# A message-passing kernel: last products and sums in two halves, fourteen groups of three, tile 1 centred ahead of the weights

## What is computed

```python
h = jnp.maximum(_layernorm(x, axis=-1), 0.0)
x_i = h[src]; x_j = h[dst]
m_ij = jax.nn.relu(jnp.concatenate([x_i, x_j], axis=1) @ W.T + b)
out = x + jax.ops.segment_sum(m_ij, src, num_segments=50000)
```

## Time and profile before

| what | value |
|---|---|
| median of 3 runs | 733.67 us (732.49 to 734.08) |
| profiled execution, its own time | 734.02 us |
| its span, first to last instruction | 732.0 us |
| mean granted clock of TensorE | 0.994 |
| busy: PE, DVE, ACT, POOL | 707.6, 628.2, 342.4, 375.0 us |

### The profile page before, as it was taken

The page is one execution under the profiler, slowest core; times in us unless marked ns, Lnnn a source line. Parts: engine busy times, 40 slices in busy tenths (PEclk is TensorE's granted clock), DMA queues, the critical chain, the costliest instruction groups (busy, mean ns, idle before and its releaser), DMA issues.

```text
span 732.0 us, 12594 instructions
## 1 busy us (share of the span) xinstructions
PE 707.6 (97%) x3466; PEld 586.6 (80%) x3466; DVE 628.2 (86%) x1868; ACT 342.4 (47%) x646; POOL 375.0 (51%) x306
## 2 busy tenths in 40 slices
PE   3999999999999999999999999999999999999995
PEld 2778888888888888888888888888888888888874
DVE  5879999889989989988988998988888888888973
ACT  4444553544445455354445535445444445454441
...
GB/s 259 383 391 358 391 372 339 374 357 353 391 339 380 343 370 371 341 386 347 349 192 141 140 144 150 152 133 162 137 143 146 137 138 147 159 154 160 86 86 73
DMA packets 36042, 182.46 MB, mean 249 GB/s; under 512 B 7019, under 2 KB 7343, under 8 KB 33049
## 3 DMA queue, kind: packets, MB, share of 16 engines
...
## 4 chain that ended last, share of the span: by engine, by line
PE 94%; DMA 2%; DVE 2%; issue 1%; another core or an unknown queue 0%; POOL 0%; ACT 0%; SPq 0%; DVEq 0%; POOLq 0%
PE z_ps L635 24%; PE z_ps L644 24%; PE z_ps L641 24%; PE ht_ps L618 11%; PE agg_ps L650 5%; PE agg_ps L651 5%; DMA ring<-w_chunks 1%; DMA xg<-x,node_i 1%; DVE ht_lo L313 1%; DVE m_lo L385 0%; DMA node_i<-node_cols 0%; POOL out L236 0%; DVE zb L334 0%; POOL xg L213 0%
## 5 line engine op out<-in xcount | busy, mean ns | idle before, releaser
L213 POOL DMA_INDIRECT xg<-x,node_i x196 | 211.3, 1078 | 245.8 <-PE ht_ps L618 201.2
L635 PE MATMUL z_ps<-w_hi,ht_hi 128*128 128x512 f32 x784 | 315.9, 403 | 1.7 <-DVE zb L323 1.5
L644 PE MATMUL z_ps<-w_hi,ht_lo 128*128 128x512 f32 x784 | 308.9, 394 | 0.0
L641 PE MATMUL z_ps<-w_lo,ht_hi 128*128 128x512 f32 x784 | 307.1, 392 | 0.0
L498 ACT CAST ht_hi<-ht_ps 128x512 fp32r<-128x512 f32 x194 | 104.7, 590 | 299.3 <-PE ht_ps L618 290.9
L236 POOL DMA_INDIRECT out<-ring,add_i x98 | 158.1, 1613 | 104.6 <-DMA out<-ring,add_i 53.3
L644 PEld LDWEIGHTS z_ps<-w_hi,ht_lo 128*128 128x128 f32 x784 | 147.8, 189 | 32.8 <-DVE ht_lo L451 0.2
L635 PEld LDWEIGHTS z_ps<-w_hi,ht_hi 128*128 128x128 f32 x784 | 148.1, 189 | 31.7 <-issue 2.8
L641 PEld LDWEIGHTS z_ps<-w_lo,ht_hi 128*128 128x128 f32 x784 | 148.1, 189 | 30.0
L313 DVE TENSOR_TENSOR ht_lo<-ht_ps,ht_hi 128x512 fp32r<-128x512 f32 x194 | 124.6, 684 | 8.1 <-ACT ht_hi L498 5.6
L505 ACT ACTIVATE xg<-xg,neg_mean 128x512 f32<-128x512 f32 x194 | 129.2, 720 | 2.0 <-DVE neg_mean L287 2.0
...
## 6 DMA issues: line engine op xcount, KB each, us to landing
out<-x SPq DMA_DIRECT2D x125, 800.0 KB
...
out<-ring,add_i POOLq DMA_INDIRECT x98
row_lanes<-src_rows ACTq DMA_DIRECT2D x49, 4.0 KB
...
```

Of the source, the lines that this page charges most:

```text
L213: nc.gpsimd.indirect_dma_start(out=xg[:, b, s, :], out_offset=None, in_=x, in_offset=bass.IndirectOffsetOnAxis(ap=node_i[:, column:column ...
L635: nc.tensor.matmul(z_ps[s][:, :], hi, w_hi[:, c, :], start=(k == 0), stop=False)
L641: nc.tensor.matmul(z_ps[s][:, :], hi, w_lo[:, c, :], start=False, stop=False)
L644: last = nc.tensor.matmul(z_ps[s][:, :], lo, w_hi[:, c, :], start=False, stop=(k == KD - 1))
```

## The change

- **Start.** VectorE takes the statistics of tile 1 after its first w_lo, ahead of tile 0's low part. ScalarE makes tile 1's deviations and centres it ahead of the high parts of weights 4 to 7. Steps 0 and 1 of both engines are written out in another order. `W_POOL` goes from 5 to 6: VectorE makes six low parts of the weights, POOL two. SyncE waits for the first gather only before the third weight load. The half sums of tile 1 go to the two banks of `agg_ps`, so its products don't wait for zb of tile 0.
- **Groups.** `TRIPLES` goes from 12 to 14, FIRST3 from 60 to 54. Eight steps leave the loops of TensorE and VectorE.
- **End.** The products of tile 97's second side, the last sums and what follows run in two halves of 256 columns, in banks of their own; ScalarE copies the first half to the ring, VectorE the second, and POOL waits for both.

```diff
--- before.py
+++ after.py
@@ -26,18 +26,19 @@
     KD = D // P
     K = SIDES * KD
     EPS = 1e-5
-    TRIPLES = 12
+    TRIPLES = 14
     FIRST3 = TILES - 2 - 3 * TRIPLES
     GROUPS = ([(f, 2) for f in range(0, FIRST3, 2)] + [(f, 3) for f in range(FIRST3, TILES - 2, 3)]
               + [(TILES - 2, 2)])
     W_LOADS = 4
-    W_POOL = 5
+    W_POOL = 6
     XS = 8
     RAMP = 4
     RING = 52
     FIRST_ADD = 56
     ROWS = 4
     LANES = 32
+    HALVES = (slice(0, OUT // 2), slice(OUT // 2, OUT))
     COPY_RUNS = 16
     COPY_ROWS = COPY_RUNS * 25
     COPIES = N // COPY_ROWS
@@ -103,6 +104,8 @@
         ht_ps = [[ps(f"ht_ps{b}{s}", [P, KD * P]) for s in range(SIDES)] for b in range(2)]
         z_ps = [ps(f"z_ps{s}", [P, OUT]) for s in range(SIDES)]
         agg_ps = [ps(f"agg_ps{b}", [P, OUT]) for b in range(2)]
+        last_z = [z_ps[1][:, HALVES[0]], ht_ps[0][0][:, HALVES[0]]]
+        last_agg = [agg_ps[0][:, HALVES[0]], ht_ps[0][1][:, HALVES[0]]]
 
         nodes_loaded = sem("nodes_loaded")
         w_loaded = [sem(f"w_loaded{n}") for n in range(W_LOADS)]
@@ -154,6 +162,10 @@
             pos = (t - FIRST3) % 3
             return pos, t - pos, 3
 
+        def half_sum(t, s):
+
+            return agg_ps[s] if isinstance(t, int) and t == 1 else z_ps[s]
+
         def sums_before(t, b):
 
             pos, first, size = place(t, b)
@@ -171,8 +183,7 @@
             for n in range(W_LOADS):
                 if n == 2:
 
-                    for side in range(SIDES):
-                        sp.wait_ge(first_arrived[side], 16)
+                    sp.wait_ge(first_arrived[0], 16)
                 ks = slice(n * K // W_LOADS, (n + 1) * K // W_LOADS)
                 sp.dma_start(ring[:, ks, :], w_of[:, ks, :]).then_inc(w_loaded[n], 16)
             sp.dma_start(bias_bc[:, :], bias.to_broadcast([P, OUT])).then_inc(bias_loaded, 16)
@@ -230,7 +241,7 @@
                     if group == len(GROUPS) - 1:
                         pool.wait_ge(add_ready, t + 1)
                     if t == TILES - 1:
-                        pool.wait_ge(last_filled, 1)
+                        pool.wait_ge(last_filled, 2)
                     else:
                         pool.wait_ge(ring_filled, t + 1)
                     nc.gpsimd.indirect_dma_start(
@@ -320,7 +331,7 @@
                 if not (isinstance(t, int) and t == 0):
                     dve.wait_ge(mlo_ready, t)
                 dve.wait_ge(half_done, t + 1)
-                nc.vector.scalar_tensor_tensor(out=zb[:, :], in0=z_ps[0][:, :], scalar=rstd[:, q, b, 0:1],
+                nc.vector.scalar_tensor_tensor(out=zb[:, :], in0=half_sum(t, 0)[:, :], scalar=rstd[:, q, b, 0:1],
                                                in1=bias_bc[:, :], op0=ALU.mult, op1=ALU.add).then_inc(half_scaled, 1)
 
             def second_half(t, m):
@@ -331,7 +342,7 @@
                 if not isinstance(t, int):
 
                     dve.wait_ge(stats_done, SIDES * (t + 4))
-                nc.vector.scalar_tensor_tensor(out=zb[:, :], in0=z_ps[1][:, :], scalar=rstd[:, q, b, 1:2],
+                nc.vector.scalar_tensor_tensor(out=zb[:, :], in0=half_sum(t, 1)[:, :], scalar=rstd[:, q, b, 1:2],
                                                in1=zb[:, :], op0=ALU.mult, op1=ALU.add).then_inc(biased, 1)
 
             def same_source(t, m):
@@ -453,28 +464,52 @@
 
             first_moments(0, first_mean)
             first_moments(1, mean_ready)
-            w_low_parts(0, 2)
+            w_low_parts(0, 1)
+            statistics(1, 1)
             first_low_part(0)
-            w_low_parts(2, 3)
+            aggregate(1, 1)
+            w_low_parts(1, KD)
             first_low_part(1)
-            w_low_parts(3, KD)
-            statistics(1, 1)
-            aggregate(1, 1)
             w_low_parts(KD, W_POOL)
+            statistics(2, 2)
+            low_parts(1, 1)
             scales(1, 0)
+            aggregate(2, 0)
             dve.wait_ge(bias_loaded, 16)
+            first_half(0, 0)
+            second_half(0, 0)
+            statistics(3, 3)
+            aggregate(3, 1)
+            low_parts(2, 0)
+            message_low(0, 0)
+            first_half(1, 1)
             dve.wait_ge(consts, 4)
             dve.wait_ge(src_cast, 8)
-            for s in range(0, 3):
-                step(s, s)
+            same_source(0, 0)
+            lanes(0, 0)
+            scales(3, 1)
+            step(2, 2)
             rounds = (FIRST3 - 2) // XS
             with dve.Fori(3, 3 + XS * (rounds - 1) + 1, XS) as s:
                 for d in range(XS):
                     step(s + d, (3 + d) % XS)
-            for s in range(3 + XS * rounds, TILES + 1):
+            for s in range(3 + XS * rounds, TILES):
                 step(s, s % XS)
-            dve.wait_ge(agg_done, TILES)
-            nc.vector.tensor_copy(ring[:, (TILES - 1) % RING, :], agg_ps[0][:, :]).then_inc(last_filled, 1)
+            m, pos = (TILES - 1) % XS, place(TILES - 1, 1)[0]
+            same_source(TILES - 1, m)
+            lanes(TILES - 1, 1)
+            dve.wait_ge(half_scaled, TILES)
+            for h, cols in enumerate(HALVES):
+                dve.wait_ge(last_product, h + 1)
+                nc.vector.scalar_tensor_tensor(out=zb[:, cols], in0=last_z[h], scalar=rstd[:, m // 2 % 2, 1, 1:2],
+                                               in1=zb[:, cols], op0=ALU.mult, op1=ALU.add).then_inc(last_biased, 1)
+                dve.wait_ge(last_high, h + 1)
+                nc.vector.scalar_tensor_tensor(out=m_lo[:, pos, cols], in0=zb[:, cols], scalar=0.0,
+                                               in1=m_hi[:, pos, cols].bitcast(F32), op0=ALU.max, op1=ALU.subtract
+                                               ).then_inc(last_low, 1)
+            dve.wait_ge(last_sum, 2)
+            nc.vector.tensor_copy(ring[:, (TILES - 1) % RING, HALVES[1]], last_agg[1]
+                                  ).then_inc(last_filled, 1)
 
         @block.scalar
         def _(act):
@@ -583,11 +618,16 @@
             first_centre(1, mean_ready)
             first_high_part(0)
             first_high_part(1)
-            w_high_parts(KD, K)
             deviations(1)
             centre(1, 1)
-            for s in range(0, 3):
-                step(s, s)
+            w_high_parts(KD, K)
+            high_parts(1, 1)
+            centre(2, 2)
+            message_high(0, 0)
+            high_parts(2, 0)
+            deviations(3)
+            centre(3, 3)
+            step(2, 2)
             with act.Fori(3, RING - XS, XS) as s:
                 for d in range(XS):
                     step(s + d, (3 + d) % XS)
@@ -603,7 +643,12 @@
                 step(s, s % XS, again=True)
             act.wait_ge(scattered, 16 * (TILES - RING))
             store_sum(TILES - 2, 1, True)
-            step(TILES, TILES % XS, again=True)
+            act.wait_ge(agg_done, sums_before(TILES - 1, 1))
+            for h, cols in enumerate(HALVES):
+                act.wait_ge(last_biased, h + 1)
+                nc.scalar.activation(m_hi[:, place(TILES - 1, 1)[0], cols], zb[:, cols], ACT.Relu).then_inc(last_high, 1)
+            act.wait_ge(last_sum, 1)
+            nc.scalar.copy(ring[:, (TILES - 1) % RING, HALVES[0]], last_agg[0]).then_inc(last_filled, 1)
 
         @block.tensor
         def _(pe):
@@ -622,8 +667,8 @@
             def products(t, b, sides=(0, 1)):
 
                 for s in sides:
-                    if not (isinstance(t, int) and t == 0):
-                        pe.wait_ge(half_scaled if s == 0 else biased, t)
+                    if not (isinstance(t, int) and t < 2):
+                        pe.wait_ge(half_scaled if s == 0 else biased, 1 if isinstance(t, int) and t == 2 else t)
                     early = isinstance(t, int) and t == 0
                     pe.wait_ge(hi_ready if early else lo_ready, SIDES * t + s + 1)
                     for k in range(KD):
@@ -632,16 +677,16 @@
                         lo = ht_lo[:, b, s, k * P:(k + 1) * P]
                         if early:
                             pe.wait_ge(w_hi_ready, c + 1)
-                        nc.tensor.matmul(z_ps[s][:, :], hi, w_hi[:, c, :], start=(k == 0), stop=False)
+                        nc.tensor.matmul(half_sum(t, s)[:, :], hi, w_hi[:, c, :], start=(k == 0), stop=False)
                         if early:
 ...
@@ -657,6 +702,8 @@
                 pe.wait_ge(same_ready, t + 2)
                 if not isinstance(t, int) or t >= 2:
                     pe.wait_ge(ring_filled, t)
+                else:
+                    pe.wait_ge(biased, 2)
                 pe.wait_ge(mlo_ready, t + 2)
                 sum_of(0, ((0, 0), (1, 1)))
                 sum_of(1, ((2, 1),))
@@ -680,17 +727,33 @@
                 pe.wait_ge(ring_filled, t)
                 pe.wait_ge(mlo_ready, t + 1)
                 sum_of(1, ((2, 1),))
-                nc.tensor.matmul(agg_ps[0][:, :], same[:, 1, :], m_hi[:, 1, :], start=True, stop=False)
```

(31 more changed lines are left out.)

11 lines of the change are left out of this document (8 added, 3 removed).

## The result

The changed kernel takes 736.48 us (median of 22 runs, 732.25 to 746.23); the kernel before, on the same chip, 733.76 (22 runs). The ratio is 1.0034 with an interval of 1.0019 to 1.0050: slower by a third of a per cent, outside the forecast range of 729.3 to 733.9. The profiled execution took 736.59 us, with a span of 734.9.

A forecast was written before the change was run, and what follows sets the result against it. TensorE's own instruction stream was taken to bound the middle, VectorE's queue the start, the compute chain the end. Start -2.5, triples +1.37 and halves -0.87 gave -2.0 us: 731.7 us against a median of 733.67, range 729.3 to 733.9.

The forecast's parts named there:

- The start: First 43 us: reordered statistics, centring and loads bring tile 3's products earlier; -2.5 us, bounds -0.5 and -3.7.
- SyncE's line: Start: weight loads about 0.7 us sooner compete with tile 1's and 2's gathers; no gain, possibly a few tenths lost.
- the bound taken for VectorE: Start: tile 2's gather, landing at about 20.1 us, limits VectorE; zb of tile 2 at 37.3 us without a stall.
- The stall: VectorE's uncaused 2.92 us wait before the first loop: taken as 2.0 us, the mean of two cases.
- TensorE's clock: Start: TensorE staying at 1.2 GHz until 23 us costs 0.7 us, of which half is charged.
- The triples: Middle: fourteen groups of three instead of twelve add six sum matmuls on TensorE, uncovered; +1.37 us.
- The add chain's part: POOL's adds: fewer pairs and more triples let add 96 start at 720.8 us and add 97 at 722.6.
- The halves: End: last products in 256-column halves, 0.122 us each, shorten the chain behind from 3.94 to 2.75 us; -0.87 us net.
- rival by which weight loads set the pace: End: each 256-column matmul takes 0.188 us instead of 0.122, making the end +0.9 us; chance 0.08.
- The floor: End: the chain of adds stops any gain beyond 4.4 us, so 729.3 us is the lowest time.
- the slower rival: End: weight loads pace the halves, +2.3 us with the triples, slower if the start gives under 0.8; chance 0.08.
- The start gives little: Rival, start: early statistics delay needed low parts, tile 2 lands later or the stall stays; net 0 to -0.8; chance 0.28.

The follow-up runs named there:

- a1: The change with SyncE waiting again for both first gathers before the third weight load; 733.68 us, ratio 1.0001 to the kernel before.
- c1: A repetition of a1, the same kernel, in another series; 731.85 us, ratio 0.9978 to the kernel before.
- d1: The change itself, run again unaltered in a later series; 741.01 us, ratio 1.0008 to the kernel before.
- a2: The kernel before with only SyncE's wait relaxed to the first gather, as in the change; 733.17 us, ratio 1.0002 to the kernel before.
- b2: As b1, but with the change's SyncE wait for the first gather alone; 731.74 us, ratio 0.9975 to the kernel before.
- d2: The change with tile 1's statistics and aggregation put behind tile 0's low parts on VectorE; 737.51 us, ratio 0.9975 to the kernel before.
- d3: The change with weights 4 to 7 put back ahead of tile 1's centring on ScalarE; 738.27 us, ratio 0.9972 to the kernel before.
- c3: The change with SyncE waiting for tile 0's and tile 1's gathers before the third weight load; 733.77 us, ratio 0.9989 to the kernel before.
- a5: The change with twelve groups of three instead of fourteen; 735.58 us, ratio 1.0027 to the kernel before.
- b1: The change with the whole start of the kernel before, keeping fourteen groups of three and the halves at the end; 731.04 us, ratio 0.9978 to the kernel before.
- d4: The kernel before, unaltered, run once more for another profile; one execution, 739.08 us.
- e1: The kernel before with fourteen groups of three and nothing else; 733.26 us, ratio 0.9986 to the kernel before.
- c2: A repetition of b1, the same kernel, in another series; 731.49 us, ratio 0.9956 to the kernel before.
- e2: A third run of the kernel of b1 and c2, beside e1; 734.40 us, ratio 0.9992 to the kernel before.
- a3: The kernel before with only the last products, sums and copies in two halves, twelve groups of three kept; 733.90 us, ratio 0.9997 to the kernel before.
- b3: The same kernel as c3, run once: the change with the third weight load only after tile 1's gathers; 733.68 us.
- c4: The kernel of b1 with the third weight load only after tile 1's gathers; 733.55 us, ratio 0.9991 to the kernel before.

## Why the prediction was wrong

**The start was forecast at -2.5 us and came out at +3.2** (P3 46.18 against 43.00). Three of its steps failed.

*SyncE's line, "no gain, and possibly a few tenths lost".* It costs S 2.8 to 3.3 us in the new order (15.54 against 12.79 and 12.22 in a1 and c1), and Z 2.3; in the repetition d1 (S 14.12, Z 24.60) it is less, 1.3 to 1.9 and 1.0. The prediction worked out when tile 2 lands and never when tile 1 does. Rows 4 began at 20.95; the statistics of tile 1, at 13.96 with no wait before them, were not among them, and a missing wait says only that the data came sooner. The edit and the new order are each harmless alone within the intervals (a2 and b2; a1 and c1) and together are the loss: the line makes tile 1 late, and the order puts tile 1 ahead of what TensorE needs first. For the same reason the bound taken for VectorE, tile 2's landing at 20.1, did not bind: the statistics of tile 2 started at 21.29 with no wait. Without the line it did: in a1 and c1 they waited for their gather until 19.67 and 19.56. And the weights 4 to 7, "covered by the same wait for tile 2" behind tile 1's centring, were made at 19.10 instead of 15.34.

*The stall, "2.0 of 2.92 us".* Treated as a length to be estimated, it is an event that occurs or not. Executions of the new order (in d2 and d3 of most of it) in which VectorE did not wait for the stall have P3 - Z between 15.4 and 16.1 us (c1 15.94, c3 15.75, d2 15.42, d3 16.08); those in which it did 18.5 to 20.3 (a5 18.52, a1 19.17, the change 20.26, d1 19.79). In the old order it is 16.3 to 17.9 without (b1 16.29, d4 16.49, b2 17.94) and 18.8 to 19.2 with (e1 18.83, before 19.17). So the forecast compared with a disturbed profile: the undisturbed start of before ends at 38.98 to 41.44 (d4, b1, c2, e2, a3), and the new order without the line and without the stall (c1) has 39.45, which lies in that range: no gain from the order is shown. The Trainium skill's page "Runtime: NRT & Kernel Launch", section "Instruction fetch mechanics", says a taken branch to a page not loaded forces a fetch and a stall. By that rule a stall should stand in every execution, at the branch; a1 and c1 are one program and only one has it.

*TensorE's clock.* The prediction priced 1.2 GHz only for the time before 23 us. With the stall in the new order TensorE idles 2.5 us before the six sums, and they run at 0.43 instead of 0.23 us: 1.2 us more, in TensorE's own path, and 0.3 more in the eight transposes behind them (1.05 instead of 0.79). Granted clock and busy times of the change, 40 to 46 us (from:to, length, busy us of PE, PEld, DVE, ACT, POOL, clock, DMA share, GB/s):

```profile
40.00:43.00 3.00, 0.57 (x2) 0.50 (x2) 2.96 (x9) 1.51 (x3) 2.40 (x2) 0.87 0.96 352
43.00:46.00 3.00, 3.00 (x12) 2.41 (x11) 2.91 (x9) 0.00 (x0) 1.19 (x2) 0.56 1.30 496
```

and c1, 37 to 43 us, without the stall:

```profile
37.00:40.00 3.00, 2.80 (x16) 2.44 (x17) 2.93 (x8) 0.70 (x2) 1.98 (x3) 1.00 1.01 381
40.00:43.00 3.00, 3.00 (x15) 2.45 (x14) 2.69 (x12) 3.00 (x7) 2.39 (x3) 1.00 0.99 367
```

Against c1, P3 of the change is 6.7 us later: 2.4 from Z (25.92 against 23.51), 2.6 from two waits of VectorE (0.96 at 38.71, and 1.67 at 31.89 for the high part that ScalarE, with a remote wait of 1.77, made at 31.27), 1.5 from the clock; 0.2 is not assigned.

**The triples: +1.37 on TensorE, right, a little high.** From P3 to the last product side: 677.35 to 677.42 us in the kernels with fourteen triples and no gap in between, 676.13 with twelve and the same end (a3): 1.26. The change's own 0.64 over before came out smaller because the profile of before had some 0.7 us of small gaps between 49 and 56 us. The add chain's part came out near: add 97 was to be possible at 722.6, and in b1, c2 and e2 the add before it went at 721.15, 721.24 and 720.63, which with 1.86 gives 722.5 to 723.1. There is some luck in it: two triples of 9.94 are 19.9 and not the 20.3 of the sum, which makes 722.2 of it and 728.9 of the floor.

**The halves: -0.87, measured -1.13.** 0.117 us per matmul instead of 0.122, and 2.63 instead of 2.75 us behind. The Trainium skill's "TensorE: Matmul & The Clock Gate", section "Back-to-back issue gap", gives 262 cycles for an isolated matmul of 256 columns, 109 ns; the trace's 117 ns lie between that and the 122 of the forecast. The rival by which weight loads set the pace is refuted.

**The floor.** The prediction had the chain of adds 1.97 us behind the compute chain in before, from one profile. In a2, a3 and d4, and with fourteen triples in b3, c4, d2 and d3, it is the chain that ends last, and it starts when the copies have ended (first add 376.2 to 385.0; 379.4 or later in these last four and in d4; d1, at 385.0, still ended with the copy). The time before is therefore not always the compute chain's: even a correct sum of the compute edits need not have been the answer.

The sign of the slower rival came true by another mechanism. *The start gives little* named the right place, tile 1's and 2's statistics ahead of low parts that TensorE needs, but doubted tile 2's landing and not tile 1's, and put its worst at -0.5. The banks and W_POOL, priced at nothing, were not tried apart.
